# One projection for four heads' queries and one for four groups' keys, laid out in bands by transfers

## The reference, cut to what matters

```python
# layer 1: D = 128, H = 16 heads, G = 4 groups, HD = 8; x is (1, 2048, 128)
q = (x @ Wq.T + bq).reshape(b, n, G, hpg, HD)      # hpg = 4 heads in a group
k = (x @ Wk.T + bk).reshape(b, n, G, HD)
v = (x @ Wv.T + bv).reshape(b, n, G, HD)
scores = jnp.einsum('bqghd,bkgd->bghqk', q, k) * scale
attn = jax.nn.softmax(scores, axis=-1)
y = jnp.einsum('bghqk,bkgd->bqghd', attn, v).reshape(b, n, d)
return y @ Wo.T + bo
```

## Time and profile before

| | |
|---|---|
| Time, 3 runs | 1390.96 us median (1389.93 to 1392.14) |
| Profiled execution: its time | 1391.06 us |
| Profiled execution: its span, first to last instruction | 1389.3 us |
| Busy in the span: PE, DVE, ACT, POOL | 91%, 77%, 59%, 10% |
| Mean granted clock of TensorE | 0.94 of full |
| q1 projections (L736) | 64 matmul records, 2 for each |
| k1 projections (L705) | 32 matmul records, 2 for each |

### The profile page before, as it was taken

The page is one execution under the profiler, slowest core; times in us unless marked ns, Lnnn a source line. Parts: engine busy times, 40 slices in busy tenths (PEclk is TensorE's granted clock), DMA queues, the critical chain, the costliest instruction groups (busy, mean ns, idle before and its releaser), DMA issues.

```text
span 1389.3 us, 19169 instructions
## 1 busy us (share of the span) xinstructions
PE 1263.5 (91%) x6358; PEld 555.3 (40%) x6358; DVE 1065.4 (77%) x2275; ACT 822.1 (59%) x1625; POOL 141.0 (10%) x259
## 2 busy tenths in 40 slices
PE   5689989999999954789999999999999999999895
PEld 3345445445443432433333443343343333334333
DVE  4667886898654558678898898999889999899524
ACT  3234436455555421178888666787666787678772
POOL 5110111103020120100000002000012000000030
PEclk8669989999999986689999999999999999999997
DMA  4010100010000000000000000000000000000000
GB/s 105 21 27 22 25 1 3 22 24 1 1 1 1 1 1 0 0 1 1 1 1 1 1 1 8 1 1 1 1 1 8 1 2 1 1 1 2 1 1 16
DMA packets 10740, 10.86 MB, mean 8 GB/s; under 512 B 2857, under 2 KB 7521, under 8 KB 10641
## 3 DMA queue, kind: packets, MB, share of 16 engines
q1 hardware_dynamic: 9632, 8.84, 2.6%
q0 software_dynamic: 1008, 0.79, 0.3%
HBM read 3.66 MB, written 1.05 MB: 3 GB/s over the span
## 4 chain that ended last, share of the span: by engine, by line
PE 70%; DVE 17%; ACT 5%; issue 5%; POOL 1%; SPq 1%; DMA 1%; DVEq 0%; POOLq 0%; ACTq 0%
PE ps L850 23%; PE ps L831 14%; PE ps L740 9%; DVE MP L1315 8%; PE ps L827 6%; PE ps L745 4%; ACT PR L1059 3%; PE ps L803 2%; PE ps L736 2%; PE ps L769 2%; PE ps L705 1%; DVE ps L1312 1%; PE ps L751 1%; PE ps L780 1%; DVE ST L1237 1%
## 5 line engine op out<-in xcount | busy, mean ns | idle before, releaser
L1059 ACT ACTIVATE PR<-ps 128x512 f32<-128x512 f32 (+2 forms) x1344 | 698.8, 586 | 381.7 <-PE ps L827 193.4
L1315 DVE TENSOR_REDUCE MP<-ps 128x1 f32<-128x512 f32 x1216 | 761.9, 683 | 118.1 <-PE ps L740 69.9
L850 PE MATMUL ps<-PR,V 128*32 128x512 f32 (+2 forms) x2688 | 433.7, 601 | 3.1 <-ACT OS L937 2.5
L740 PE MATMUL ps<-KO,Q 64*128 64x512 f32 x1024 | 379.9, 459 | 14.2 <-DVE MP L1315 7.3
L831 PE MATMUL ps<-Q,KO 64*128 64x512 f32 x1024 | 343.7, 446 | 10.2 <-DMA Q<-MR 6.0
L831 PEld LDWEIGHTS ps<-Q,KO 64*128 64x128 f32 x1024 | 160.2, 186 | 297.4 <-issue 128.4
L740 PEld LDWEIGHTS ps<-KO,Q 64*128 64x128 f32 x1024 | 170.4, 189 | 90.1 <-DVE MP L1315 35.9
L745 PE MATMUL ps<-KO,QO 96*128 96x512 f32 (+2 forms) x320 | 124.3, 436 | 23.0 <-DVE QO L1296 10.0
L827 PE MATMUL ps<-QO,KO 97*128 97x512 f32 (+3 forms) x320 | 140.3, 454 | 4.1 <-DMA QO<-MR 2.4
L850 PEld LDWEIGHTS ps<-PR,V 128*32 128x32 f32 (+1 forms) x2688 | 74.1, 115 | 128.2 <-issue 61.4
L827 PEld LDWEIGHTS ps<-QO,KO 97*128 97x128 f32 x320 | 61.0, 197 | 130.9 <-issue 80.3
(11 more groups left out here) (211 smaller groups left out, 772.3 us busy)
## 6 DMA issues: line engine op xcount, KB each, us to landing
QO<-Q SPq DMA_DIRECT2D x72, 64.0 KB, 2.0
Q<-MR SPq DMA_DIRECT2D x64, 2.0 KB
result<-V SPq DMA_DIRECT2D x4, 256.0 KB, 2.3
H<-in_L_attn_wq SPq DMA_DIRECT2D x1, 512.0 KB, 3.4
HQT<-in_L_attn_wo SPq DMA_DIRECT2D x1, 512.0 KB, 5.8
ew<-in_L_ffn_expert_w POOLq DMA_DIRECT2D x1, 512.0 KB, 4.2
bq<-in_L_attn_bq POOLq DMA_DIRECT2D x12, 0.1 KB, 3.4
wd<-in_L_ffn_w_down SPq DMA_DIRECT2D x1, 176.0 KB, 4.8
```

Source lines behind the costliest of these rows:

```text
L740: last = nc.tensor.matmul(bank[:, :], Q1[rows, buf, h // 2, q * P:(q + 1) * P], KO1[rows, g, kc * QC:(kc + 1) * QC], start=True, stop=True)
L850: nc.tensor.matmul(dst, VO[layer][:, kt, g, :], PR[:, u % NP_RING, q0:QC], start=kt == 0, stop=kt == key_tiles(layer, c) - 1).then_inc(pv_ ...
L1059: nc.scalar.activation(PR[:, u % NP_RING, q0:QC], ps[:, bank_of_score[u], q0:QC], ACT.Exp, scale=SCALE[layer]).then_inc(exp_done, 1)
L1315: v.tensor_reduce(MP[:, buf, h, q, kc:kc + 1], bank[:, 0:w], AX, ALU.max).then_inc(free, 1)
```

## The change

All four heads of a group now come from one projection and so do the keys of all four groups of a chunk, each in a block of 32 rows (24 of the three copies, one for the maxima, 7 empty). There are 16 "q1" and 4 "k1". The split parts are written to a staging tile `QS` of two buffers instead of `Q1` and `KO1`, and SP moves blocks of 32 rows from there: four transfers for a "q1", sixteen for a "k1" (each group's block goes to rows 0, 32, 64 and 96 of `KO1`), counted on a new semaphore `spread`. The matmuls of maxima and scores stay as they are, 64 rows each; the upper 32 rows of a query band are set to zero by POOL beforehand. PE's "max" waits on `spread` instead of `tailed`, and needs the one step `("k1",)`, whatever its group. Before a staging buffer is written, ACT waits for the transfers of the step before the last; SP waits for all earlier spreads before it issues the next.

```diff
         def queries(layer, c, g, it):
             if layer:
-                return [("q1", g, c, it, pair) for pair in range(PAIRS)]
+                return [("q1", g, c, it)]
...
-            return out + gaps("6 6 7 6 6 1 1 1 1", [("hqT", QT - 1), ("down", c), ("norm1", c), ("x2T", c)]
-                              + [("k1", g, c) for g in range(G1)] + [("v1", c)])
+            return out + gaps("6 6 7 6 6 1", [("hqT", QT - 1), ("down", c), ("norm1", c), ("x2T", c)]
+                              + [("k1", c), ("v1", c)])
...
-                return [("q0", b), ("k0", g)] if layer == 0 else [("q1", b, h // 2), ("k1", g)]
+                return [("q0", b), ("k0", g)] if layer == 0 else [("q1", b), ("k1",)]
...
+        staged, spread_by = {}, [0]
+        for step in program:
+            if step[0] in ("q1", "k1"):
+                staged[step] = len(staged)
+                spread_by.append(spread_by[-1] + 16 * (HG if step[0] == "q1" else 4 * G1))
...
+                    if step in staged:
+
+                        if by_pool(step):
+                            sp.wait_ge(tailed, lows)
+                        else:
+                            sp.wait_ge(*released(k))
+                        part, now = QS[:, staged[step] % 2, :].bitcast(f32), spread_by[staged[step]]
+                        if now:
+
+                            sp.wait_ge(spread, now)
+                        else:
+                            sp.wait_ge(blank, 1)
+                            sp.dma_start(eb, A["L1_ffn_expert_b"]).then_inc(ld["biases"], 16)
+                        for n_part in range(P // HEAD_ROWS):
+                            rows = part[n_part * HEAD_ROWS:(n_part + 1) * HEAD_ROWS, :]
+                            if step[0] == "q1":
+                                row = band_of(n_part).start
+                                dst = Q1[row:row + HEAD_ROWS, step[3], n_part // 2, :]
+                                sp.dma_start(dst.bitcast(f32), rows).then_inc(spread, 16)
+                                continue
+                            for row in range(0, P, HEAD_ROWS):
+                                dst = KO1[row:row + HEAD_ROWS, n_part, step[1] * QC:(step[1] + 1) * QC]
+                                sp.dma_start(dst.bitcast(f32), rows).then_inc(spread, 16)
...
-                        if name in tails_at:
-
-                            pe.wait_ge(tailed, tails_at[name])
+                        if name in spread_at:
+
+                            pe.wait_ge(spread, spread_at[name])
...
+                    if staged[item] > 1:
+
+                        act.wait_ge(spread, spread_by[staged[item] - 1])
                     i = nc.scalar.activation(dst, bank, ACT.Identity, bias=low_bias, scale=low)
...
+            for it in (0, 1, 3):
+                nc.gpsimd.memset(Q1[:, it, :, :].bitcast(f32), 0.0)
+            nc.gpsimd.engine_nop().then_inc(blank, 1)
...
-            v.memset(WQ13[:, :, :, :, :], 0.0)
-            v.memset(WK13[:, :, :, :], 0.0).then_inc(cleared, 1)
+            v.memset(WQ13[:, :, :, :], 0.0)
+            v.memset(WK13[:, :, :], 0.0).then_inc(cleared, 1)
```

More of the change, by code:

```diff
@@ L53 @@
 PAIRS = HG // 2
+HEAD_ROWS = P // HG
 CONST_W = P + 10
@@ L179, in build @@
         ROW = ((6, 7, 0, 1, 2, 3), (5, 6, 7, 0, 1, 2, 3))
-        ld = {n: sem("loaded_" + n) for n in ("x", "query", "keys", "attn0", "ffn0", "attn1", "moe", "const", "masks")}
+        ld = {n: sem("loaded_" + n) for n in ("x", "query", "keys", "attn0", "ffn0", "attn1", "moe", "biases", "const", "masks")}
         side_full = sem("side_full")
@@ L195, in build @@
         pv_done = sem("pv_done")
+        spread = sem("spread")
+        blank = sem("blank")
         clipped = sem("clipped")
@@ L421, in steps0 @@
                     begun = [step for _, step in behind[1:QUANT_STAGES]]
-                    beside = queries(1, 0, 0, 0) + begun[:1] + maxima(1, 0, 0, 0, range(NC - 2))
-                    begun, behind = begun[1:], behind[:1] + behind[QUANT_STAGES:]
+                    beside = queries(1, 0, 0, 0) + begun[:2] + maxima(1, 0, 0, 0, range(NC - 2))
+                    begun, behind = begun[2:], behind[:1] + behind[QUANT_STAGES:]
                 yield from iteration(0, c, g, beside, behind, outs, carry, it, begun)
@@ L482, in facing @@
                     j, near = i, 0
-                    while here is not None and out[j][2] % 2 != here and near < APART:
+                    while here is not None and near < APART and out[j][2] % 2 != here:
                         j = next(n for n in range(j + 1, len(out)) if out[n][0] in ("max", "row_max", "q1", "k1"))
@@ L734, in side_item @@
                 elif kind == "q1":
-                    g, c, _, pair = item[1:]
-                    last = nc.tensor.matmul(bank[:, :], WQ13[:, g, pair, :, :], XT[:, c * QC:(c + 1) * QC], start=True, stop=True)
+                    g, c, _ = item[1:]
+                    last = nc.tensor.matmul(bank[:, :], WQ13[:, g, :, :], XT[:, c * QC:(c + 1) * QC], start=True, stop=True)
                 elif kind == "max" and item[1] == 1:
@@ L950, in side_item @@
                     if kind == "q1":
-                        g, _, it, pair = item[1:]
-                        i = nc.scalar.activation(Q1[:, it, pair, :], bank, ACT.Identity, bias=bq_low[:, pair, g:g + 1],
-                                                 scale=low_q)
+                        dst, _, low_bias, low = of_parts(item)
+                        act.wait_ge(spread, spread_by[staged[item] - 1])
+                        i = nc.scalar.activation(dst, bank, ACT.Identity, bias=low_bias, scale=low)
                     elif by_dma(item):
@@ L1019, in side_item @@
                         own = slice(r * HD1, (r + 1) * HD1)
-                        for pair in range(PAIRS):
-                            copy(WQ13[:, :, pair, :, own],
-                                 bank[:, 0:P].rearrange("p (g a b d) -> p g a b d", g=G1, a=PAIRS, b=2)[:, :, pair, :, :])
-                        i = copy(WK13[:, :, :, own], bank[:, 2 * P:2 * P + LAT].rearrange("p (g d) -> p g d", g=G1)
-                                 .unsqueeze(2).broadcast_to([P, G1, 2, HD1]))
+                        copy(WQ13[:, :, :, own], bank[:, 0:P].rearrange("p (g h d) -> p g h d", g=G1, h=HG))
+                        i = copy(WK13[:, :, own], bank[:, 2 * P:2 * P + LAT].rearrange("p (g d) -> p g d", g=G1))
                 elif kind == "shift":
@@ L1165, in walk @@
                         pool.wait_ge(*released(k))
+                        if step[0] == "q1" and step[3] == 2:
+                            pool.wait_ge(q_moved, MOVES * sum(by_dma(s) for s in steps))
+                            for band in range(2):
+                                rows = slice(band * BAND + HEAD_ROWS, (band + 1) * BAND)
+                                nc.gpsimd.memset(Q1[rows, 2, :, :].bitcast(f32), 0.0).then_inc(blank, 1)
+                                pool.wait_ge(blank, 2 + band)
                         dst = of_parts(step)[0]
```

92 lines of the change are left out of this document (45 added, 47 removed).

## The result

The changed kernel takes 1379.98 us, median of 4 runs (1379.13 to 1382.11), where the kernel before, on the same chip, took 1391.55. The ratio is 0.992, with a 95% interval of 0.9902 to 0.9937: 11.6 us faster, where 6.6 were forecast.

A forecast was written before the change was run, and what follows sets the result against it. PE bounds layer 1, DVE close behind; between the layers DVE's maxima and rounding run one after another. Terms -0.6, -3.5, -2.6, -1.3, -16.3, +8.2, +4.0, +5.5 sum to -6.6: 1391.06 becomes 1384.5 us, range 1373 to 1395.

The forecast's parts named there:

- A: Stretch up to the last shift of layer 0; the prediction's terms there come to -6.7 us.
- B: Stretch from layer 0's last shift to layer 1's first; the prediction's terms there come to +16.4 us.
- C: Stretch from layer 1's first shift to the end of the span; predicted -16.3 us.
- Issue as the price of a spread: Sixteen transfers issued by SP cost 11.6 us from the end of the subtraction to PE, where nothing covers them.
- The rival of hidden issue: Issuing costs little, both key waits are 9.3 us shorter and the clock holds: near 1362 us, chance 0.03.
- Keys of chunk 2: Between the layers, PE waits uncovered for the spread: net +8.2 us, and +4.0 for PE's clock falling after idling.
- Keys of chunk 3: Between the layers, the maximum behind the values' projection starts at 586.6 in place of 581.1: +5.5 us.
- Layer 1: Fourteen query pairs become single projections, winning 18.9 us, net -16.3, with their transfers costing nothing.
- the term for neighbours: In layer 1, 13 fewer neighbouring matmuls use different bands, at 0.2 us each: a loss of 2.6 us.
- The rival that ACT's and DVE's legs count as well: In layer 1, PE's and DVE's legs both count every time, 25.5 in place of 18.9: 1378 us, chance 0.15.
- The rival that DVE takes over: In layer 1, removing PE's leg only exposes DVE, each projection worth 0.67 us: sum +2.9, 1394 us, chance 0.14.
- Layer 0: Start -0.6, keys of chunks 0 and 1 -3.5 and -2.6; a rival has layer 0 giving nothing, 1391.8, chance 0.18.

The follow-up runs named there:

- eight: The changed kernel with 8 transfers per key projection in place of 16, the rows behind each block zeroed at the start by POOL: 1377.4 us.
- split: The changed kernel with the same 16 transfers for the keys of chunks 2 and 3, half of them issued by POOL: 1375.0 us.
- filler: The changed kernel with 58 more unused matmuls on PE just ahead of its wait for chunk 2's keys: 1381.9 us.
- twice: The changed kernel with each of layer 1's 14 query projections done twice in a row on PE: 1394.84 us.
- between: The changed kernel with layer 1's 14 query projections done twice, the second between a score and a maxima matmul of different bands: 1401.75 us.
- q_only: The changed kernel with the keys' projections as before, so only the queries are changed: 1371.69 us.
- k_only: The changed kernel with queries in pairs as before, so only the keys are changed: 1409.12 us.
- early: The changed kernel with 8 transfers per key projection, maxima waiting only for their own chunk's keys, and POOL's zeroing between its weight loads: 1367.78 us.

## Why the prediction was right, and where its steps were off

By the stretches of the table, the prediction's terms are -6.7 for A, +16.4 for B and -16.3 for C, in sum -6.6. The two traces have -6.6, +15.0 and -20.3, in sum -11.9. So what was missed is 4.0 us in C and 1.4 in B, and the size of the first is not certain (below).

**Issue as the price of a spread: right.** 11.6 us were predicted from the end of the subtraction to PE, 11.5 measured, and sixteen issues in 10.00. eight and split show that it is the issues. The rival of hidden issue is out.

**Keys of chunk 2: right in sum.** Predicted +8.2 and +4.0 for the clock, 12.2. "y0" is 4.2 us late where the last shift of layer 0 was 6.6 early, so 10.8 were lost in between; with the 1.3 that the first queries were to give there, that is 12.1. Its second part, the clock, has the right size (PE needs 11.4 us from its return to "y0", for 8.8 before, 1.9 of which went away) but the cause that was given, PE's idleness, is not confirmed: filler took the idleness away and not the low clock.

**Keys of chunk 3: right.** Predicted +5.5. POOL's first subtraction ends at 577.84 for 574.98 before, 2.9 us later, and DVE's maxima start 8.4 us later: +5.6. Between "y0" and that subtraction 1.4 us were won, for which the prediction has no term.

**Layer 1: the main term right, the term for neighbours wrong.** Predicted 18.9 - 2.6 = 16.3, measured 20.3; against the other nine traces of the same layer 1 it is 14.9 to 20.4, so 16.3 is not outside what was measured. The term that the rows don't bear out is the loss of 2.6 us for thirteen fewer neighbours in different bands. PE's rows by form over the same steps, 593 to 1218 before:

```profile
L740 PE MATMUL ps<-KO,Q 64*128 64x512 f32 x803 | 295.9, 449 | 4.9 <-DVE MP L1315 2.5 <-ACT PR L1059 0.6
L831 PE MATMUL ps<-Q,KO 64*128 64x512 f32 x824 | 285.3, 445 | 7.0 <-DMA Q<-MR 3.2 <-DVE MP L1315 2.4
...
L736 PE MATMUL ps<-XT,WQ 128*128 128x512 f32 x52 | 28.9, 638 | 1.6 <-ACT PR L1059 1.5
```

and 601 to 1206 after:

```profile
L771 PE MATMUL ps<-KO,Q 64*128 64x512 f32 x803 | 292.3, 449 | 4.0 <-DVE MP L1354 2.6 <-ACT PR L1090 0.6
L863 PE MATMUL ps<-Q,KO 64*128 64x512 f32 x824 | 275.0, 438 | 7.8 <-DVE MP L1354 4.1 <-DMA Q<-MR 3.2
...
L767 PE MATMUL ps<-XT,WQ 128*128 128x512 f32 x26 | 14.4, 637 | 1.5 <-ACT PR L1090 1.5
```

The projections account for 14.5 us of the 20.9 that PE is less busy. The rest is in the same number of scores and maxima. They were to become dearer by 2.6 and have become cheaper, by 10.3 and 3.6 us of time that partly overlaps; in the other traces with one projection the scores take 275 to 277 us as well. Why is open. It may be that a projection over all 128 rows breaks the run of 64-row matmuls in two and ends an overlap on both sides, which a count of pairs leaves out. The medians of twice and between agree with that, their rows don't, since a projection put between a score and a maximum left both as they were; none was put back between two scores, where by the prediction the removed one often stood. Of the gain in C some 15 us are PE's own time (14.9 by twice's median, 14.5 by the rows), and the rest, up to 5 us, is not shown. The rival that ACT's and DVE's legs count as well (1378, measured 1380.0) is not ruled out: both lost an instruction for each projection, and no kernel tried those alone.

**The rival that DVE takes over is out.** The iterations are 43.0 and 43.1 us long (875.22 to 918.20 to 961.34), for 44.3, with 43.2 predicted. Its turning point was worked out wrong: with the prediction's other terms the sum is zero where a projection is worth 12.3 / 14 = 0.88 us before the loss of neighbours, and not 0.67, where it stands at +2.9 already.

**Layer 0: the sum holds in this trace, its parts don't stand.** Predicted -6.7 up to the last shift, measured 6.6. But the changed kernel's A is the shortest of the six traces of that program; by the others the gain is 2.9 to 5.3 us. And q_only, which leaves the keys as they were, has A 4.3 us below before, and k_only, which changes them, 1.8. That the keys of chunks 0 and 1 gave 6.1 us is therefore not shown, and the close fit of the sum is in part luck. By the medians k_only loses 18.2 us, for 17.1 in B, which leaves nothing won elsewhere by the keys; the changed kernel stands 8.3 us above q_only, for the same 17.1 in B, which leaves 8.8. The two don't agree, and this stays open.

## What to carry to other kernels

Price a transfer by its issue where several go out together, and look at what the first instruction that waits for them holds up: the same merging that was right in the queries' case, with most of an iteration as cover, cost 17 us between the layers in the keys' case with none. Before spreading a result over bands, ask which copies are needed at all, and let each consumer wait for its own part. And test the halves of a change apart: here one half alone gained 19 us and the other alone lost 18, and the whole, at -12, passed for a small success.

## What the runs showed of the hardware

While POOL's memsets ran, DVE's tensor_scalar, cast and copy did not end (5.02 us for 0.17, 11.43 for 0.16, 12.45 for 1.34), while tensor_tensor and the masked maximum read from PSUM, and tensor_reduce, ran at full pace beside them. The Trainium skill ("SBUF — State Buffer", Who interferes with whom) has this rule: a VectorE instruction of those kinds can take a pair of ports that it shares with GpSimd, and whichever comes second is blocked for the whole of the other. The tensor_scalar agrees with it, issued at 28.13 us behind a memset that ran from 26.18 to 33.12. The cast of early, whose row begins ahead of the memset's and which was held all the same, agrees in kind but not in order. 4 us of a kernel hung on it.

TensorE's clock fell to its lower level behind a stretch of 12 us at 1.00 in which PE was busy for 10.22, with 1.73 us of idleness between: 0.57 over the next 8 us. And POOL's issues of 64 KB transfers were shorter than SP's, 0.50 against 0.63 us.
